# Norm, ranks and weighing reordered on VectorE, a convolution moved to GpSimd, and the first expert pair and the plan laid out differently

## The reference

```python
x = x + xattn(layernorm(x), ctx_1024)     # 16 heads of 16, 257 context rows per batch
x = x + mamba(layernorm(x))               # W_in, conv of 4 taps, dt, cumulated decays, W_out
x = x + moe(layernorm(x))                 # 8 experts of 704, top 2, softmax of the two logits

# inside mamba: every batch uses the mix of batch 0, divided by its own norm
dt = softplus(dt + dt_bias); A = A_param * dt
cumA = cumsum(A, axis=1)
norm = exp(cumA) * cumsum(exp(-cumA), axis=1)
out = ssd(x, A, B, C)[0] / norm

# inside moe
for e in range(8):
    h = silu(xf @ w_gate[e]) * (xf @ w_up[e])
    out = out + gates[:, e:e+1] * (h @ w_down[e])
```

## Time and profile before

| | us |
|---|---|
| median of three runs | 1454.3 |
| the profiled execution | 1450.36 |
| its span in the trace | 1448.6 |
| TensorE busy | 1359.7 (94%) |
| VectorE busy | 1066.1 (74%) |
| ScalarE busy | 962.8 (66%) |
| GpSimd busy | 769.6 (53%) |
| GpSimd's scatter waiting for the scatter before it | 113.2 in 28 waits |

### The profile page before, as it was taken

The page is one execution under the profiler, slowest core; times in us unless marked ns, Lnnn a source line. Parts: engine busy times, 40 slices in busy tenths (PEclk is TensorE's granted clock), DMA queues, the critical chain, the costliest instruction groups (busy, mean ns, idle before and its releaser), DMA issues. The chain is left out here.

```text
span 1448.6 us, 53361 instructions
## 1 busy us (share of the span) xinstructions
PE 1359.7 (94%) x16654; PEld 1232.5 (85%) x16654; DVE 1066.1 (74%) x4217; ACT 962.8 (66%) x2683; POOL 769.6 (53%) x1345
## 2 busy tenths in 40 slices
PE   7979999999999999999999999689999999998997
PEld 6858888888888888888888888689889899998997
DVE  4657788888778878878888887566667766666775
ACT  4637777777767767777777776456757566666664
POOL 4515656656655665665566565434444454543554
PEclk9979999999999999999999999899999999999999
DMA  6212544554433333343333332335545555555786
GB/s 195 68 38 72 183 144 141 173 163 136 124 98 95 97 120 97 98 121 94 95 108 112 93 92 64 122 108 133 166 125 159 158 172 147 157 168 164 221 255 191
DMA packets 94235, 190.71 MB, mean 132 GB/s; under 512 B 18480, under 2 KB 60976, under 8 KB 88592
## 3 DMA queue, kind: packets, MB, share of 16 engines
q1 hardware_dynamic: 78448, 170.64, 36.1%
q0 software_dynamic: 15680, 18.76, 7.4%
HBM read 158.92 MB, written 31.65 MB: 132 GB/s over the span
## 5 line engine op out<-in xcount | busy, mean ns | idle before, releaser
L606 PE MATMUL sc<-late_room 128*128 128x256 f32 (+1 forms) x2578 | 351.6, 292 | 26.2 <-DVE late_hidden L1969 13.9
L606 PEld LDWEIGHTS sc<-late_room 128*128 128x128 f32 x2578 | 329.4, 194 | 34.0 <-issue 23.5
L1145 ACT ACTIVATE early_room<-early_room,nmx 128x257 f32<-128x257 f32 x512 | 255.7, 502 | 70.0 <-DVE nmx L1482 59.8
L1482 DVE CUSTOM_DVE_ANT_0 early_room<-sc,early_room 128x257 f32<-128x257 f32 x512 | 192.4, 422 | 75.9 <-PE sc L606 69.0
L1121 ACT ACTIVATE early_room<-v_p 128x512 f32<-128x512 f32 x256 | 152.7, 596 | 138.8 <-PE km L606 116.8
L2193 POOL TENSOR_TENSOR ctx_lo<-ctx,ctx_hi 128x516 fp32r<-128x516 f32 x128 | 166.6, 1302 | 103.5 <-ACT ctx_hi L1121 103.5
L2292 POOL DMA_INDIRECT out<-late_rows,oi x56 | 90.7, 1620 | 167.8 <-DMA out<-late_rows,oi 113.2
L606 PE MATMUL km<-ctx_hi,wkh 128*128 128x256 f32 x512 | 160.3, 313 | 0.6 <-ACT rp L1121 0.4
L606 PE MATMUL km<-ctx_lo,wkh 128*128 128x256 f32 x512 | 146.0, 285 | 0.0
L606 PE MATMUL km<-ctx_hi,wkl 128*128 128x256 f32 x512 | 145.5, 284 | 0.0
L606 PE MATMUL v_p<-wvh,ctx_hi 128*128 128x256 f32 x512 | 144.1, 281 | 0.0
(11 more groups left out here) (260 smaller groups left out, 3548.1 us busy)
## 6 DMA issues: line engine op xcount, KB each, us to landing
late_room<-d_split SPq DMA_DIRECT2D x43, 1536.0 KB
ctx<-in_ctx SPq DMA_DIRECT2D x128, 258.0 KB, 2.8
early_room<-in_mask SPq DMA_DIRECT2D x512, 32.1 KB, 1.7
d_split<-pieces SPq DMA_DIRECT2D x24, 512.0 KB
pieces<-in_wd SPq DMA_DIRECT2D x24, 256.0 KB
wg<-in_wg SPq DMA_DIRECT2D x8, 704.0 KB
wu<-in_wu SPq DMA_DIRECT2D x8, 704.0 KB
early_room<-in_x SPq DMA_DIRECT2D x32, 128.0 KB, 2.0
```

What stands on the lines that cost most here:

```text
L606: return nc.tensor.matmul(out, lhsT, rhs, start=start, stop=stop)
L1145: nc.scalar.activation(pr[:, g, :], sm[:, g, :], ACT.Exp, bias=nmx[:, g:g + 1], scale=-1.0, accum_out=rsum[:, g:g + 1]).then_inc(exp_done, 1)
L1482: V.tensor_tensor_reduce(sm[:, g, :], SC[g][:, 0:S], msk[:, b, :], -1.0, 3.0e38, ALU.add, ALU.min, nmx[:, g:g + 1]).then_inc(max_done, 1)
```

## The change

1. At `b == 0` VectorE runs `weigh` and `attention_out` ahead of `reciprocals`; `statistics1` moves to `b == 2`. `norms` is cut in two: the product that reads PSUM goes between the two head pieces, the reciprocal behind `take_ranks`. `project_out` waits for `ranked` (the instruction that reads the ranks) and no longer for the one behind it.
2. The convolution runs on GpSimd, in its tile 1, `b == 3`, ahead of that batch's `split_low`. `ssd_mix` makes 16 small matmuls in place of 64; ScalarE copies the result to `ys`, and four identity matmuls spread it.
3. In the last batch of the last tile VectorE runs `low_z` of pair 0 first and `low_b` of pair 0 before the heads, ScalarE `high_b` of pair 0 before `take_rp`. The last tile's `expand_last`, `weigh` and `attention_out` go from `ending_a(0)` to `ending_b(0)`. The loads of down weights of pairs 0 and 1 wait for chunks of pair 0.
4. In the pair stage GpSimd copies `oi` of the pair before ahead of the gather.
5. The 29 plan steps are cut into six parts of 4 or 5, at pairs 12 to 15.

```diff
             def ssd_mix():
                 pe.wait_ge(norm_done, 1)
-                pe.wait_ge(ssd_dve, SSD_C)
+                pe.wait_ge(ssd_conv_done, SSD_C)
...
                 for h in range(H):
-                    for b in range(TB):
-                        last = mm(M[b * Q:(b + 1) * Q, h * HD:(h + 1) * HD], ws[:, h, :], xs[:, h * HD:(h + 1) * HD])
+                    last = mm(M[0:Q, h * HD:(h + 1) * HD], ws[:, h, :], xs[:, h * HD:(h + 1) * HD])
                 last.then_inc(ssd_pe, 1)
                 pe.wait_ge(ssd_act, 3)
+                for b in range(TB):
+                    last = mm(M[b * Q:(b + 1) * Q, 0:D], ident[0:Q, 0:Q], ys)
+                last.then_inc(ssd_pe, 1)
...
                     if runs(i - 3):
-                        pe.wait_ge(chosen_done, i - 1)
+                        pe.wait_ge(ranked, i - 2)
...
             def load_pair(p):
                 if p == 0:
                     sp.wait_ge(twin_out, 16)
                     sp.wait_ge(v_ready, B)
+                    sp.wait_ge(gu_ready, 2)
                 if p == 1:
                     sp.wait_ge(o_ready, B)
+                    sp.wait_ge(gu_ready, FC)
...
             def to_keys(i, b):
+                if last_batch(i, b):
+                    low_z(0, 0)
...
             def from_reciprocals(i, b):
+                if b == 0 and runs(i - 1):
+                    weigh(i - 1)
+                    attention_out(i - 1)
                 if runs(nxt[0]):
                     reciprocals(*nxt)
...
-                if b == 0 and runs(i - 1):
-                    weigh(i - 1)
-                    attention_out(i - 1)
-                if b == 0 and runs(i + 2):
-                    statistics1(i + 2)
...
-                if runs(i):
+                if runs(i) and not last_batch(i, b):
                     first_head(i, b)
                 if pick_now:
                     select_index(i - 2)
-                if runs(i):
+                if b == 0 and runs(i - 2):
+                    sum_of_decays(i - 2)
+                if runs(i) and not last_batch(i, b):
                     second_head(i, b)
-                if b == 3 and isinstance(i, int) and i == NT - 1:
-                    low_z(0, 0)
                 if soft_now:
                     softplus_end(i - 1)
+                if last_batch(i, b):
+                    e = V.value_load(pair_expert(0), min_val=0, max_val=E - 1)
+                    low_b(0, e, 0)
+                    low_b(0, e, 1)
+                    take_output(i, b)
...
-                if b == 0 and runs(i - 2):
-                    norms(i - 2)
                 if b == 0 and runs(i - 3):
                     take_ranks(i - 3)
+                if b == 0 and runs(i - 2):
+                    inverse_norm(i - 2)
...
+                if b == 2 and runs(i + 2):
+                    statistics1(i + 2)
...
+            def ssd_conv():                       # on GpSimd
+                pool.wait_ge(ssd_dve, SSD_X)
+                conv_step(G.tensor_tensor(cv[:, 0], xp[:, :, 0:Q], tap(0), ALU.mult))
+                for n in range(1, KC):
+                    conv_step(G.tensor_tensor(cv[:, 1], xp[:, :, n:n + Q], tap(n), ALU.mult))
+                    conv_step(G.tensor_tensor(cv[:, 0], cv[:, 0], cv[:, 1], ALU.add))
...
             def tile(i, k=None):                  # GpSimd
                 for b in range(TB):
...
+                    if b == 3 and isinstance(i, int) and i == 1:
+                        ssd_conv()
                     if runs(three[0]):
                         split_low(*three)
...
             def body2(p, s):                      # GpSimd
                 if p == 0:
                     add_bias(NT - 1)
+                else:
+                    pair_owners(oi[:, 1 - s], p - 1, oi_done)
                 if p < NPAIR - 2:
                     gather_pair(p + 2, s)
...
                 if p > 0:
-                    pair_owners(oi[:, 1 - s], p - 1, oi_done)
                     scatter_pair(p - 1, 1 - s)
```

More of the change, by code:

```diff
@@ L1196, in ssd_out @@
                 act.wait_ge(ssd_pe, 5)
+                copy(ys, M[0:Q, 0:D]).then_inc(ssd_act, 1)
+                act.wait_ge(ssd_pe, 6)
                 copy(y0[:, :], M[:, 0:D]).then_inc(ssd_act, 1)
@@ L1249, in tile @@
                         ssd_out()
-                    if b != 0 and runs(i):
+                    if b == 3 and isinstance(i, int) and i == NT - 1:
+                        e = nc.scalar.value_load(pair_expert(0), min_val=0, max_val=E - 1)
+                        high_b(0, e, 0)
+                        high_b(0, e, 1)
+                    elif b != 0 and runs(i):
                         take_rp(i, b)
@@ L1329, in early @@
                     gate_exp(NT - 3)
+                else:
+                    high_b(p, e, 0)
                 silu2(p, 0)
-                high_b(p, e, 1)
+                if p == 0:
+                    take_rp(NT - 1, TB - 1)
+                else:
+                    high_b(p, e, 1)
                 high_h(p, s, 0)
@@ L1615, in norms, with sum_of_decays @@
             def norms(j):
+                sum_of_decays(j)
+                inverse_norm(j)
+            def sum_of_decays(j):
                 dve.wait_ge(c2_ready, j + 1)
@@ L1835, in ssd_weights, with last_batch @@
                 ssd_step(V.tensor_tensor(ws, gs, ls, ALU.mult))
-                dve.wait_ge(ssd_act, 3)
+                dve.wait_ge(ssd_act, 4)
+            def last_batch(i, b):
+                return b == TB - 1 and isinstance(i, int) and i == NT - 1
             def to_keys(i, b):
@@ L1977, in early @@
                 e = V.value_load(pair_expert(p), min_val=0, max_val=E - 1)
-                low_b(p, e, 0)
+                if p > 0:
+                    low_b(p, e, 0)
                 gate_up2(p, 0)
-                low_b(p, e, 1)
+                if p > 0:
+                    low_b(p, e, 1)
                 low_h(p, s, 0)
@@ L2025, in ending_b @@
                     take_ranks(NT - 3)
+                    weigh(NT - 1)
+                    attention_out(NT - 1)
                     scale_y(NT - 2)
@@ L2218, in last_probs, with conv_step, tap @@
                                     .broadcast_to([P, NG, NH, 2]), ALU.mult).then_inc(px_done, 1)
+            conv_steps = [0]
+            def conv_step(ins):
+                conv_steps[0] += 1
+                ins.then_inc(ssd_conv_done, 1)
+                pool.wait_ge(ssd_conv_done, conv_steps[0])
+            def ssd_conv():
+                pool.wait_ge(ssd_dve, SSD_X)
+                pool.wait_ge(par_in, 16)
+                taps = prm("convw").rearrange("p (c k) -> p c k", k=KC)
+                def tap(n):
+                    return taps[:, :, n:n + 1].broadcast_to([P, NC, Q])
+                conv_step(G.tensor_tensor(cv[:, 0], xp[:, :, 0:Q], tap(0), ALU.mult))
+                for n in range(1, KC):
+                    conv_step(G.tensor_tensor(cv[:, 1], xp[:, :, n:n + Q], tap(n), ALU.mult))
+                    conv_step(G.tensor_tensor(cv[:, 0], cv[:, 0], cv[:, 1], ALU.add))
+                conv_step(G.tensor_tensor(cT, cv[:, 0], prm("convb").unsqueeze(2).broadcast_to([P, NC, Q]), ALU.add))
+                n8 = P // HD
+                for a in range(NH):
+                    last = G.tensor_tensor(cbd[:, a], cT[:, a, :].unsqueeze(1).broadcast_to([P, n8, Q]),
+                                           cst("bm8").unsqueeze(2).broadcast_to([P, n8, Q]), ALU.mult)
+                conv_step(last)
+                assert conv_steps[0] == SSD_C
             def add_bias(j):
```

123 lines of the change are left out of this document (57 added, 66 removed).

## The result

| | before | after |
|---|---|---|
| median of four runs | 1452.98 | 1407.24 |
| lowest to highest | 1450.34 to 1455.21 | 1405.49 to 1409.27 |
| span of the profiled execution | 1448.6 | 1405.7 |

The ratio is 0.9686, with a 95% interval of 0.9664 to 0.9709: 45.7 us faster. The forecast was 1414 and the range 1403 to 1430. The time fell well inside the range, but some terms of the sum came out for other reasons than the prediction gave, and the experiments found that the time of the kernel before depends on the chip, so that some 17 of the 45.7 us are there on one chip and not on another.

What follows compares the result with a forecast made beforehand. TensorE's order, busy 94% of the span, was taken as the floor, so only closing its gaps gains. +2.5 − 19 − 7 − 15 = −38.5 gave 1411.9 from the profiled 1450.36, 1415.8 from the median; forecast 1414, range 1403 to 1430.

Steps and rivals of the forecast that it cites:

- Term B: Tiles, before `project_out`: reordering VectorE's row closes the gap behind the scores; −19 us, bounds 0 to −21.3.
- The room of 0.3: Tiles: VectorE has read the ranks at 741.2, TensorE ends the scores at 741.53, so 0.3 us to spare.
- the sum of 14 × 1.11 + 13 × 0.44: Lost time before `project_out`: 14 tiles losing 1.11 us and 13 losing 0.44, 21.3 us in all.
- Term A: Mix of batch 0: convolution to GpSimd and fewer small matmuls; +2.5 us, bounds −6 to +8.
- The prediction's queue: GpSimd, tile 1: convolution of 6.0 us ahead of `split_low`, so TensorE stands 4.5 us and `expand` comes at about 91.
- Term C: Start of the pairs: TensorE's gaps of 5.38 and 2.52 us in pair 0 go, less costs; −7, bounds 0 to −10.
- Term D: Pair stage: earlier copy of `oi` and the plan cut into parts; −15 us, bounds −3 to −20.
- (a): Rival, tiles: VectorE's gap before `project_out` only halves, −9 in place of −19; 1424, chance 0.13.
- (b): Rival, pairs: the wait for `oi` becomes one for the scatter's DMA, −7 in place of −15; 1422, chance 0.12.
- (c): Rival, tile 1: GpSimd's queue costs more, steps of 0.8 and a longer cold clock, +8; 1420, chance 0.07.
- (d): Rival, tiles: the later softmax reciprocal delays GpSimd and ScalarE's next exponentials, every tile lengthens; 1459, chance 0.03.
- (e): Rival, whole kernel: gains and new stalls cancel; 1452, chance 0.03.

Runs made afterwards that it cites:

- b_all: Changed kernel with the order at `b == 0` undone (reciprocals, weighing, statistics, norms, wait for `chosen_done` as before): 1415.57, ratio 0.9869.
- ctl_after: The changed kernel itself, no edit, run again on another chip: 1405.44, ratio 0.9796.
- ctl_before: The kernel before itself, no edit, run again on another chip: 1434.12.
- b_weigh: Changed kernel with the weighing alone back behind the softmax reciprocal: 1406.18, ratio 0.9812.
- late_old: Changed kernel with the old order at `b == 0`, plus an unused VectorE reduction ahead of the first row maximum in the loop's tiles: 1431.77, ratio 0.9880.
- late_new: Changed kernel plus an unused VectorE reduction ahead of the first row maximum in the loop's tiles: 1406.77, ratio 0.9712.
- a_d_plan: Changed kernel with the convolution back on VectorE and the plan's last 29 steps in two rows at pairs 12 and 13: 1404.31, ratio 0.9692.
- c_all: Changed kernel with `low_z`, `low_b`, `high_b`, the last weighing and the waits of the down weights' loads as before: 1410.47, ratio 0.9824.

## Why the prediction was right

**Term B, the gap before `project_out`, forecast −19, measured −20.8.** The mechanism is shown: what VectorE had in a row set the gap, and the gap closes in every tile and opens again in b_all. The room of 0.3 was 0.5. But the sum of 14 × 1.11 + 13 × 0.44 took the rhythm of one profile for a property of the kernel. Where no tile is long the same edit is worth 8 to 10: the stage from the `project_out` at 102 to the last takes 795.7 in b_all and 787.3 in ctl_after, and the medians are 10 apart, with before at 1433 and 1434. From ctl_before to ctl_after the row of the table that gave −20.8 gives −9.5. So the size of −19 was right only where the first maximum is as late as in the profile that it was read from. The rest is insurance against that lateness, which under the old order costs 0.77 in a long tile. The whole change is worth 3.1% on one chip and 2.0% (ratio 0.9796) on another, and both are right. Of the two things that the prediction let share the gap, the 0.60 of the statistics and the weighing behind the reciprocal, the traces have the first in every tile and the second in long ones only. The order of the weighing by itself was undone only where no tile is long (b_weigh, nothing); on a chip with long tiles only part 1 as a whole was (late_old against late_new, 25 us), so what the weighing alone is worth there is not shown.

What makes the first maximum late is not shown. The trace of before puts the idle time on the scores in most tiles and on "issue" in four, though the scores are long done; it is 0.36 on two chips and 0.77 or 1.5 on the others in the same instruction. That it is the first one of the loop's body suggests the jump, but late_old and late_new speak against the plain form of that: there the added instruction is the first of the body and starts without any idle time (707.87), and the idle time stands between it and the maximum. No experiment took that apart.

**Term A, the mix, forecast +2.5, measured +0.5.** One profile does not fix this term: between ctl_before and ctl_after the same stretch grew by 2.4 (99.71 to 102.09). The prediction's queue was right in kind, and each of its sizes within 0.8: the copy came 1.2 earlier than before (done 77.21), the convolution took 6.7 from its start at 77.29 where 6.0 was said, `split_low` followed, and TensorE stood 5.30 where 4.5 was said; these rows are of GpSimd and TensorE of after:

```profile
77.29 1.01 POOL L2257 TENSOR_TENSOR wg<-wg,par 128x192 f32<-128x192 f32 x1 [6.34 <-DVE wg L1834]
78.39 0.52 POOL L2259 TENSOR_TENSOR wg<-wg,par 128x192 f32<-128x192 f32 x1
78.98 0.60 POOL L2260 TENSOR_TENSOR wg<-wg 128x192 f32<-128x192 f32 x1
84.03 1.27 POOL L2214 TENSOR_TENSOR ctx_lo<-ctx,ctx_hi 128x516 fp32r<-128x516 f32 x1
```

```profile
85.36 0.58 PE L609 MATMUL km<-ctx_hi,wkh 128*128 128x256 f32 x1 [5.30 <-POOL ctx_lo L2214]
90.70 0.50 PE L609 MATMUL sc<-rp,spread 32*128 32x128 f32 x8
93.07 1.05 PE L609 MATMUL km<-wg 128*32 128x256 f32 x4 [0.51 <-DVE dtv L1638]
95.76 1.18 PE L609 MATMUL km<-wg 32*32 32x16 f32 x32 [0.46 <-ACT wg L1127]
```

`expand` at 90.70 is what the prediction said (about 91), 4.7 later than before. The mix behind it then got 4.2 shorter, and there the step failed that took 2.5 for 48 small matmuls, less 1.3 for the copy and the spreading (1.2, which the sum writes as 1.5; its 1.2 for VectorE is worked out from no row). From the first small matmul to the first instruction behind the mix before took 4.17 us (94.31 to 98.48); with 16 of them, the new copy and the spreading a_d_plan takes 3.93 (90.81 to 94.74). What got shorter is the wait ahead of it, here of the kernel before, for the product of the norm that part 1 moved forward:

```profile
90.55 1.92 PE L606 MATMUL km<-wg 128*32 128x256 f32 x4 [2.31 <-DVE dtv L1618]
```

2.31 became 0.51 (0.27 in a_d_plan): one part of the change paid for another, and my sum looked at each alone. Of the rest, 0.9 is the clock: the four matmuls take 1.92 at a granted clock of 0.50 and 1.05 at 1.00, and the small ones behind them ran at 0.50 in before too. The move to GpSimd by itself costs 3.7: 5 of standing, less what VectorE gains.

**Term C, start of the pairs, forecast −7, measured −3.8.** The gaps of 5.38 and 2.52 are gone, in after three pieces of 0.53, 0.25 and 0.35 and nothing in their place; ctl_after still has 0.77 and 1.31. Given back: the weighing, priced at its length of 1.5, cost TensorE a wait of 1.61 in pair 1 (at 925.20), where before had 0.31, and in this profile the clock was not saved, as the 1 to 2 of my term had it: twelve matmuls at 910.07 took 2.76, where ctl_after took 1.60. Pair 0 took 10.16 there and 6.72 in ctl_after. The down weights were never waited for. Measured by undoing it is 3.8 too in the trace of c_all, and 5.0 by the medians. So the mechanism stood, and the step that failed is the price of what was added: the weighing's wait, and the clock.

**Term D, the pairs, forecast −15, measured −16.6.** The sum was near although its terms were not: `oi` was said to be 12 and is 16.3 when undone alone, the plan was said to be 3 and is 2, and the two together, 18, are more than the whole stage gained here (16.6) or from ctl_before to ctl_after (16.1). They share something, so the nearness is in part luck. The step that failed is the first sentence of the prediction on bounds, that a steady pair is filled to the brim: the ten pairs from 1176.15 took 128.5 and now take 124.7, and the last pair behind them 14.45 and now 12.42. A busy share of 100% did not prove TensorE to be the bound; the ends of matmuls in a trace are modelled, and the same 18 matmuls of one pair are put down at 2.48 us in before (at 1206.30) and at 2.32 in after (at 1170.80).

**The rivals.** (a), the gap only halves: no, 0.62 everywhere. (b), the wait for `oi` becomes one for the scatter: it does once in the pairs (1.00 at 1130.33) and twice just behind them (0.89 and 1.04), and nowhere else. (c), a costlier queue: 0.8 more standing, no more. (d), a later reciprocal: no; in the tile of 210.98 it stood at 209.63, 1.35 before `project_out` as in every tile, and nothing behind it ran late. (e): no. Of the signs that the prediction named, two did not come: pairs 0 and 1 took 10.16 and 18.76 in place of 13 to 15, and in ctl_after a wait over 1 us (1.31) is left before the third chunk of pair 0.

## What to carry to other kernels

Before a gap is priced by the tiles in which it shows, find what divides the long tiles from the short ones; if it is one instruction that comes late on some chips and not on others, the edit's worth is that of the steady gap plus insurance. A delay put in by hand can show both, but only on a chip that does not have the lateness by itself; look first whether the idle time was there anyway. Edits of one row of instructions share one room: their prices add neither one by one nor at zero. And where an engine shows 100%, look for a ring through the other engines (here a copy behind two gathers, ScalarE, a scatter) whose round is just over that engine's own work.

## What the hardware showed

- GpSimd took 0.51 to 0.60 us for 192 columns where VectorE took 0.36. The Trainium skill, GPSIMD Engine Reference, "Elementwise — side-by-side cycle accounting", has it about two times slower at 2048 elements; these runs have 1.4 to 1.7.
- Sharing goes both ways: VectorE's addition of two SBUF operands took 1.33 beside GpSimd's `split_low` in a_d_plan (1.34 in the earlier trace rows), and GpSimd's first multiplication took 1.01 in place of 0.52 while VectorE's product of two SBUF operands ran (77.25 to 77.93 in after). Both agree with the lock of the Trainium skill, SBUF — State Buffer, "SBUF: two separate sides"; in the second it is GpSimd that waits.
- The same program of one core has two medians by chip, 1433 to 1434 and 1450 to 1453, with nearly the same granted clock (0.988 and 0.984 in the two profiles of before). Of the 21.3 us between these profiles 13.7 lie in the attention stage, where one instruction, the first of VectorE's loop, starts 0.84 after the scores on one chip and mostly 1.2 to 2.0 on the other.
